# A recommender tower: ten one-hot features instead of eight, one buffer of vectors with placing copies, ids spread two items ahead

## The reference

```python
combined = concatenate([dense[:, None, :], e], axis=1)            # 2048 x 27 x 128
inter = einsum('bnd,bmd->bnm', combined, combined)[:, I, J]       # pairs, 351
h = concatenate([dense, inter, dense], axis=1)                    # 607
h = maximum(h @ W_top1 + b_top1, 0); h = maximum(h @ W_top2 + b_top2, 0); y = h @ W_top3
```

## Time and profile before

| | |
|---|---|
| median of 3 runs | 590.69 us (590.42 to 593.9) |
| the profiled execution | 589.59 us, its span 587.5 us |
| mean granted TensorE clock | 0.916 of full speed |
| busy: PE, DVE, ACT, POOL | 465.1, 317.5, 206.3, 280.9 us |
| DMA, mean | 46 GB/s |

### The profile page before, as it was taken

How to read it: one execution, slowest core, us unless ns; L and a number is a source line. 1 busy time by engine, 2 the same in 40 slices (tenths; PEclk the granted TensorE clock), 3 DMA queues, 4 the chain that set the end, 5 groups by cost and what they waited for, 6 DMA issues and landing times. The chain is left out here.

```text
span 587.5 us, 11290 instructions
## 1 busy us (share of the span) xinstructions
PE 465.1 (79%) x4081; PEld 410.4 (70%) x4081; DVE 317.5 (54%) x733; ACT 206.3 (35%) x708; POOL 280.9 (48%) x298
## 2 busy tenths in 40 slices
PE   1748867898888978797687959879887958886667
PEld 1637756788777977687576858668776857765556
DVE  5445885645566655646465546545665635634140
ACT  2112352333443343335143333423542343334231
POOL 8742345554555545445554555545455545555100
PEclk9999898797899998899799977979899978999689
DMA  8910021111111111111111111111111111111000
GB/s 218 259 39 19 24 73 38 37 42 37 38 37 37 42 42 37 36 40 37 41 37 43 37 32 42 42 43 40 36 38 37 41 37 37 40 38 37 18 1 1
DMA packets 17307, 27.21 MB, mean 46 GB/s; under 512 B 8561, under 2 KB 11121, under 8 KB 17241
## 3 DMA queue, kind: packets, MB, share of 16 engines
q0 software_dynamic: 9216, 18.89, 11.2%
q1 hardware_dynamic: 8034, 7.54, 5.0%
HBM read 26.40 MB, written 0.01 MB: 45 GB/s over the span
## 5 line engine op out<-in xcount | busy, mean ns | idle before, releaser
L271 POOL DMA_INDIRECT rows<-in_tbl,idx x288 | 277.8, 964 | 266.8 <-DMA rows<-in_tbl,idx 161.9
L633 DVE TENSOR_TENSOR onehot<-ids_ps,row_of 125x1024 fp32r<-125x1024 f32 x130 | 153.0, 1218 | 87.9 <-PE ids_ps L341 58.9
L356 PE MATMUL fetch_ps<-onehot,t_hi 125*128 125x256 f32 x512 | 157.1, 331 | 50.9 <-ACT vecs L504 17.4
L356 PEld LDWEIGHTS fetch_ps<-onehot,t_hi 125*128 125x128 f32 x512 | 114.8, 224 | 62.4 <-issue 36.9
L356 PE MATMUL fetch_ps<-onehot,t_lo 125*128 125x256 f32 x512 | 154.0, 326 | 1.3 <-issue 1.3
L691 DVE COPY_PREDICATED inter<-mask,dots_ps 27x64 f32<-27x64 int32 (+2 forms) x512 | 106.0, 207 | 87.1 <-ACT inter L533 72.2
L533 ACT COPY inter<-dots_ps 27x64 f32<-27x64 f32 (+1 forms) x512 | 102.1, 199 | 113.8 <-remote 58.8
L333 PE MATMUL dots_ps<-vecs 128*64 128x54 f32 x2048 | 131.7, 227 | 6.4 <-issue 5.1
L333 PEld LDWEIGHTS dots_ps<-vecs 128*64 128x64 f32 x2048 | 123.8, 141 | 14.2 <-issue 8.1
L356 PEld LDWEIGHTS fetch_ps<-onehot,t_lo 125*128 125x128 f32 x512 | 114.4, 223 | 8.4 <-issue 4.9
L504 ACT COPY vecs<-fetch_ps 128x256 f32<-128x256 f32 x64 | 38.7, 605 | 175.8 <-PE fetch_ps L356 107.7
(11 more groups left out here) (39 smaller groups left out, 162.1 us busy)
## 6 DMA issues: line engine op xcount, KB each, us to landing
rows<-in_tbl,idx POOLq DMA_INDIRECT x288
vecs<-in_tbl SPq DMA_DIRECT2D x8, 448.0 KB
rows<-in_r_dense_features SPq DMA_DIRECT2D x16, 64.0 KB
h_sb<-in_W_top_laid SPq DMA_DIRECT2D x2, 512.0 KB, 3.5
w_sb<-in_W_top SPq DMA_DIRECT2D x1, 512.0 KB
vecs<-in_tbl SPq DMA_DIRECT2D x8, 52.0 KB
idx<-in_ids SPq DMA_DIRECT2D x16, 13.0 KB
h_sb<-in_W_top_laid SPq DMA_DIRECT2D x1, 256.0 KB
```

The costliest lines, as they stand in the source:

```text
L271: nc.gpsimd.indirect_dma_start(out=rows[v % 2][:, s, :], out_offset=None, in_=tables[f - 1][:, :], in_offset=bass.IndirectOffsetOnAxis(ap= ...
L356: last = pe.matmul(fetch_ps, part[0:KP, k, h * KH + t, :], onehot[buf][h][0:KP, t, :], start=(h == 0 and t == 0 and part is t_hi), stop=(h ...
L633: dve.tensor_tensor(onehot[buf][h][0:KP], ids_ps[0:KP].rearrange("p (o r) -> p o r", o=1).to_broadcast([KP, KH, R]), row_of[0:KP, h * KH:( ...
```

## The change

Features 2 and 8, with tables of 1250 rows (10 blocks of 125), are fetched by one-hot too; their items come first and have 20 matmuls. A tile has 16 gathers and 17 transposes left, in groups of 3, 4, 4, 4 and 2 vectors. `vecs` is one buffer for one round; fetched items are copied to a new buffer `found` [128, 10, 256], contiguously, and at the head of the next step ScalarE copies them to `vecs` in two *placing* copies, one per tile (`place`), each after the dots that read that tile's place last and before item 0 is copied to `found`. Groups 0, 2, 4 of a tile are always copied by ScalarE, 1 and 3 by VectorE. The ids of item k + 2 are spread within item k; the first comparison of the next round stands before the last split. Item 3 stands between a tile's transposes 0, 1 and layer 1's last part, items stand around each half of layer 2, and the last two items around layer 3. The second dense weights have their own buffer, so GpSimd no longer waits for their sum; tile 0's groups wait for each other. SP waits for the first two tables' conversion before it loads `W_top1`; the output goes in two DMAs. The diff, its core:

```diff
+SPREAD = (2, 8, 1, 5, 6, 9, 14, 18, 24, 26)
+
+AT_ONCE = 4
 
...
-    groups = [list(range(a, min(a + 4, NR))) for a in range(0, NR, 4)]
+    groups = [list(range(a, b)) for a, b in ((0, 3), (3, 7), (7, 11), (11, 15), (15, 17))]
...
+    KP = 125
+    KT = [tables[f - 1].shape[0] // KP for f in SPREAD]
+    KH = [kt // 2 for kt in KT]
...
-        vecs = [sb(f"vecs{s}", [P, 2, P, NP]) for s in range(2)]
+        vecs = sb("vecs", [P, 2, P, NP])
+
+        found = sb("found", [P, X, R])
...
-        w_dense2 = rows[1][:, NR - 4:NR, :].rearrange("p s d -> p (s d)")
...
+        w_dense2 = sb("w_dense2", [P, H1])
...
+            sp.wait_ge(hi_made, 2)
+            sp.wait_ge(lo_made, 2)
...
+            by_round = out.rearrange("(i r n) o -> o r i n", r=2, n=R)
+            for r in range(2):
+                sp.dma_start(by_round[:, r], y_sb[r * LATE:r * LATE + 1].rearrange("p (i n) -> p i n", n=R)).then_inc(
+                    out_written, 16)
+            sp.wait_ge(out_written, 32)
...
-                    if k == NG - 2 and first and v == 1:
-
-                        pool.wait_ge(dense_w_sum, 1)
...
-                        if not (first and v == 0):
-                            pool.wait_ge(gathered[vv % 2][kk], ii * (32 * n) + (vv // 2 + 1) * 16 * n)
+                        pool.wait_ge(gathered[vv % 2][kk], ii * (32 * n) + (vv // 2 + 1) * 16 * n)
                     pool.sem_inc(groups_begun, 1)
-                    for s in mine:
+                    landed = i * (32 * len(mine)) + v // 2 * (16 * len(mine))
+                    for n, s in enumerate(mine):
                         f = ORDER[s]
+                        if n and n % AT_ONCE == 0:
+
+                            pool.wait_ge(gathered[v % 2][k], landed + 16 * n)
+                            pool.sem_inc(gathers_resumed, 1)
                         nc.gpsimd.indirect_dma_start(
...
-            def fetch_item(i, r, k):
-                spread = {0: 1, 1: 3, 3: 4, 4: 6, 6: 8}
-                fetch(k, *item(i, r, k), spread_of(i, r, spread[k]) if k in spread else None)
+
+            def fetch_items(i, r, *ks):
+                for k in ks:
+                    ahead = {0: 1, X - 1: None}.get(k, k + 2)
+                    fetch(k, *item(i, r, k), spread_of(i, r, ahead) if ahead else None)
...
-                        if k == 4:
+                        if k == X - 4:
                             pe.wait_ge(ident_made, 1)
-                        if k >= 4:
-                            transpose_rows(i, v, (k - 4,))
+                        if k >= X - 4:
+                            transpose_rows(i, v, (k - X + 4,))
                     transpose_rows(i, v, (4,))
-                    fetch_item(i, r, 0)
+                    fetch_items(i, r, 0)
                 dots(i, v, 0, spread_of(i, r, 2))
-                fetch_item(i, r, 1)
-                if prev:
-                    layer1(*prev, 1)
-                    layer1(*prev, 2)
+                fetch_items(i, r, 1)
+                if prev:
+                    layer1(*prev, 1, 2)
                 else:
                     transpose_rows(i, v + 1, (0, 1))
-                fetch_item(i, r, 2)
+                fetch_items(i, r, 2)
                 dots(i, v, 1)
                 if prev:
                     transpose_rows(i, v + 1, (0, 1))
+                fetch_items(i, r, 3)
+                if prev:
                     layer1(*prev, 3)
                 transpose_rows(i, v + 1, (2, 3, 4))
-                fetch_item(i, r, 3)
-                dots(i, v + 1, 0, spread_of(i, r, 5))
-                fetch_item(i, r, 4)
+                fetch_items(i, r, 4)
+                dots(i, v + 1, 0)
+                fetch_items(i, r, 5)
                 if prev:
                     layer2(*prev, 0)
-                fetch_item(i, r, 5)
-                dots(i, v + 1, 1, spread_of(i, r, 7))
-                fetch_item(i, r, 6)
+                fetch_items(i, r, 6)
                 if prev:
                     layer2(*prev, 1)
-                fetch_item(i, r, 7)
+                fetch_items(i, r, 7)
+                dots(i, v + 1, 1)
+                fetch_items(i, r, 8)
                 if prev:
                     layer3(*prev)
+                fetch_items(i, r, 9)
...
-            def copy_fetched(slot, k, m):
+            def copy_fetched(k, m):
                 act.wait_ge(onehot_used, m * 2 + 2)
-                nc.scalar.copy(vecs[slot][:, :, :, NR + k],
-                               fetch_ps.rearrange("p (t b) -> p t b", t=2)).then_inc(fetched, 1)
+                nc.scalar.copy(found[:, k, :], fetch_ps).then_inc(fetched, 1)
 
             def copy_items(i, r, *ks):
                 for k in ks:
-                    copy_fetched((r + 1) % 2, k, item(i, r, k)[0])
+                    if k == 0:
+
+                        act.wait_ge(placed, i * 4 + r * 2 + 2)
+                    copy_fetched(k, item(i, r, k)[0])
+
+            def place(i, r, t):
+                if not (static(i) and i == 0 and r == 0):
+
+                    act.wait_ge(dots_done, i * (8 * UNITS) + r * (4 * UNITS) - (1 - t) * 2 * UNITS)
+                if t == 0:
+                    act.wait_ge(fetched, i * (2 * X) + (r + 1) * X)
+                nc.scalar.copy(vecs[:, t, :, NR:N],
+                               found[:, :, t * P:(t + 1) * P].rearrange("p k b -> p b k")).then_inc(placed, 1)
...
+                    place(i, r, 0)
                     take_vectors(i, v, 0)
+                    place(i, r, 1)
                     copy_items(i, r, 0)
                     take_vectors(i, v, 2, 4)
                     rectify1(*prev, 0)
...
+                    act.wait_ge(lo_made, X)
+                    place(i, r, 0)
+                    place(i, r, 1)
                     take_vectors(i, v, 4)
                     copy_items(i, r, 0)
...
                 if prev:
                     rectify1(*prev, 1, 2)
                 else:
-                    take_vectors(i, v + 1, 1)
+                    take_vectors(i, v + 1, 0)
+                    split(X)
                 copy_items(i, r, 2)
                 take_products(i, v, 1)
                 if prev:
-                    take_vectors(i, v + 1, 1)
+                    take_vectors(i, v + 1, 0)
+                copy_items(i, r, 3)
+                if prev:
                     rectify1(*prev, 3)
                 else:
+                    split(X + 1)
+                split_input(i, v)
+                take_vectors(i, v + 1, 2, 4)
+                copy_items(i, r, 4)
+                take_products(i, v + 1, 0)
+                copy_items(i, r, 5)
+                if prev:
+                    rectify2(*prev, 0)
+                copy_items(i, r, 6)
+                if prev:
+                    rectify2(*prev, 1)
+                else:
                     split(X + 2)
-                split_input(i, v)
-                take_vectors(i, v + 1, 3)
-                copy_items(i, r, 3)
-                take_products(i, v + 1, 0)
-                copy_items(i, r, 4)
-                if prev:
-                    rectify2(*prev, 0)
-                copy_items(i, r, 5)
+                copy_items(i, r, 7)
                 take_products(i, v + 1, 1)
-                copy_items(i, r, 6)
-                if prev:
-                    rectify2(*prev, 1)
+                copy_items(i, r, 8)
                 split_input(i, v + 1)
-                copy_items(i, r, 7)
+                copy_items(i, r, 9)
...
-                    take_vectors(i, v, 1, 3)
-                    compare_items(i, r, 1, 2)
+                    take_vectors(i, v, 1)
+                    compare_items(i, r, 1)
+                    take_vectors(i, v, 3)
+                    compare_items(i, r, 2)
                 else:
-                    compare(0, 0)
+                    compare(0, 0, 0)
                     make_mask()
-                    dve.tensor_copy(ids_t[:, R:B], ids_i[:, R:B]).then_inc(ids_cast, 1)
+                    dve.tensor_copy(ids_t[:, R:B // 2], ids_i[0:X, R:])
+                    dve.tensor_copy(ids_t[:, B // 2:B], ids_i[LATE:LATE + X, :]).then_inc(ids_cast, 1)
                     for k in range(X):
                         split(k)
                         if k + 1 < X:
-                            compare(k + 1, (k + 1) % 2)
-                        if k == 6:
+                            compare(k + 1, k + 1, (k + 1) % 2)
+                        if k == X - 3:
+
+                            dve.wait_ge(lo_made, 6)
                             take_vectors(i, v, 1)
-
                     dve.wait_ge(lo_made, X)
-                    dve.memset(vecs[1][:, :, :, N:], 0.0)
-                    sum_dense_weights()
+                    dve.memset(vecs[:, :, :, N:], 0.0).then_inc(pads_zero, 1)
                     compare_items(i, r, 0)
                     take_vectors(i, v, 3)
                     compare_items(i, r, 1, 2)
+                merge_products(i, v, 0)
+                compare_items(i, r, 3)
```

(77 more changed lines are left out.)

116 lines of the change are left out of this document (59 added, 57 removed).

## The result

The changed kernel takes 609.0 us (median of 4, 605.1 to 611.6), the kernel before, run beside it, 590.6: a ratio of 1.030, 95% interval 1.023 to 1.037. The profiled execution took 607.9 us, its span is 606.4. This holds for the chip of these runs. On another chip the same changed kernel is faster than the kernel before, and that is the main finding.

A forecast was written before the change was run, and what follows sets the result against it. Gathers (67.0 us a step) and TensorE run nearly level before; after, TensorE alone sets the pace at 67.1. Span 587.5 + 18 (start) + 7 (steps) - 5 (end) = 607.5, plus 2.1 around it: 609 us, range 582 to 623.

The forecast's parts named there:

- the start: Two more table conversions before the first tile: tile 0 transposed at 80.4 us instead of 66.3, +14.1 us.
- the first step: Tile 0's to tile 2's transposes: placing copies +1.5, fetching +5.3, less about 3 us of wait; tile 2 18 us later.
- the end: Tile 15's gather waits go, -6 us, and the placing copies give 1 back: -5 us.
- TensorE's work: Per step, eight items of 16 matmuls become eight of 16 and two of 20, less four transposes: +5.3 us.
- Own step before: TensorE's two-tile step in the kernel before, without gather waits and 1.1 us of slow clock: 62.8 us.
- (a): Item 3 between transposes and layer 1's last part covers the wait for vector copies: -1.6 us a step, 0.5 kept.
- (c): Waits for fetched items behind product copies, 2.7 us a step: less cover at the second place, +0.5, up to +0.9.
- (b): Ids two items ahead and next round's comparison moved earlier take the one-hot wait away: -0.8 us a step.
- The placing copy: ScalarE's 128x1280 copy at a step's head takes 1.8 us, between 1.2 and 2.4, adding 0.9 us per step.
- rival (2): Clock: 4.4 us a step of work lost at 1.2 GHz goes with the gather waits; 589 us, chance 0.125.
- Rival (1): Reordering removes 3.6 us a step more of TensorE's waits for other engines; 588 us, chance 0.125.
- (4): Slower still: placing copies at 2.4 us or more and waits at their upper ends; 625 us, chance 0.15.

## Why the prediction was right

The forecast was 609 us and the measured median is 609.0. The mechanism is the one named: the bound passes from the gathers to TensorE, whose step is 67.4 us (forecast 67.1). That it hits to the microsecond is luck. The sum gave a span of 607.5 us and it was 606.4, from terms that were off by more: the start by -6.5 us, the first step by +9.2, the six steps by +1.9 and the end by -5.7.

- *Gathers out of the way*: right. No wait of PE for rows from 140 us on; the last gathers are issued at 543.5, before tile 14 is transposed.
- *TensorE's work, +5.3 us; net of waits +4.3*: near. On the second chip, without stalls and with loosened gathers, the two kernels' steps are 330.3 / 6 = 55.0 and 358.2 / 6 = 59.7 us, a difference of 4.7. TensorE's busy time in six steps on the fourth chip is 302.9 us in the kernel before with loosened gathers, at a granted clock of 1.00, and 335.6 in the changed one, at 0.99: 5.4 a step, for the forecast's 5.3.
- *Own step before, 62.8 us*: not tested where it was read. The 54.2 us of another chip don't refute it, since the changed kernel's step differs by 7.4 between the chips; adding that gives an estimate of 61.6.
- *Waits*: (a) the wait for VectorE's copy went, but group 4's for ScalarE came in both tiles of a step, 20.7 / 6 = 3.4 us where I had 0.9 + 0.5. (c) I kept 3.2 us for fetched items, and 6.9 / 6 = 1.2 was left. (b) 0.6 of the one-hot waits stayed. In sum 5.2 against 4.6 us, besides 2.8 us of short waits put down to "issue".
- *The placing copy*: the upper end, 2.47 us, and not the middle that I took; the row that reads SBUF with a stride (L528) was the one to go by. The Trainium skill's rule (SBUF — State Buffer, The DMA port swizzle), extra cost for every new line of 16 bytes, fits in its direction: 2.47 us for reads 1 KB apart against 1.27 for reads without a gap.
- *The clock*: part of rival (2) did happen. Over the six steps the granted clock is 0.96, before it was 0.92. With +5.3 us of work the busy time grew by only 3.3 a step, so the clock gave back about 2.0 us (an estimate), where I had 1.1. The waits took that back: idle time fell by 1.8 us a step, where I had 2.0 for gathers and 1.0 for the rest. So a step grew by 1.5 us where I had 1.2.
- *The start*: forecast +14.1 for tile 0, measured +7.6. So tile 0 was ready before 75 us, which the prediction had set as a sign of being wrong. The step that failed is that I added two turns to the whole of before's start. That had a stall in it which did not come back:

```profile
32.57 2.35 DVE L633 TENSOR_TENSOR onehot<-ids_ps,row_of 125x1024 fp32r<-125x1024 f32 x2 [7.37 <-remote]
```

  A turn's usual wait there is 2.7 us, so 4.7 us were the stall's. Three of the changed kernel's turns have a shorter wait there, 2.41, 1.65 and 2.11 us, which gives most of the rest. The turns themselves are as worked out: items start at 13.16 and 20.58, 7.4 us for ten blocks (7.5 by my terms).
- *The first step*: +13.1 where I had 18 - 14.1 = 3.9. Two placing copies in series are 4.83 us, and dots start 5.2 us after tile 0's transposes instead of 2.4. TensorE is idle for 2.3 us before them, and they ran mostly at the low level of the clock. In the whole first step its busy time is 58.2 us against 48.8 before, 9.3 more where I had 5.3, at a granted clock of 0.83 against 0.86. The changed kernel's stretch of them, granted clock third from the right, is this, where it was 1.00 before:

```profile
79.00:87.00 8.00, 7.89 (x71) 7.46 (x72) 3.89 (x10) 2.89 (x15) 2.99 (x4) 0.57 0.09 26
```

- *The end*: -10.7 against -5. From tile 14's last transpose to tile 15's it is 19.6 us after, 30.3 before: besides the 6.0 us of gather waits another 5 of short waits in that stretch went.
- *The other signs*: no wait for gathered rows, tiles 67.4 us apart, and VectorE and ScalarE busier came as listed. GpSimd's long idle time before a tile's first gathers came only in part, 3.5 to 4.6 us at the last three tiles against 2.3 before, and the profile puts it down to "issue" and not to transposes.
- *Rival (1)* (the reordering takes the waits away, 588 us) did not come on this chip. Of *(4)* the first condition came, a placing copy of over 2.4 us, but not its 625 us. On the fourth chip a case came for which no rival stood: ScalarE's stalls absent altogether. I read ScalarE's idle time with no engine as cause and took it as the kernel's, though it comes and goes with the chip or the occasion. My prediction holds where the stalls are there as in the trace that it was read from.

## What to carry to other kernels

Where two chains have nearly the same length, a change that trades one for the other can be decided by what the trace can't ascribe to the kernel. Look at idle time with no engine behind it, and ask for a second chip before a variant is believed. The kernel that such a trade starts from may allow a better remedy: on the chips without stalls the gathers needed one more group in flight, not two features fewer. And compare variants side by side only: 562 us for an edit that gives nothing looked like a gain of 47.

## What the runs showed of the hardware that was not expected

- Stalls come and go with the chip or the occasion: on the first and third chip, ScalarE stood idle with the releaser "remote" for 51 to 94 us in each of six traced executions, in pauses of mostly 3 to 4 us, and VectorE for 2 to 32 us more; on the second and fourth, in eight traced kernels, not once. The changed kernel took 601 to 609 us with them and 562 without. The kernel before took 587 to 591 us everywhere, as one would expect if its gathers set its pace. The instruction queue moved the same for the same program on each (0.66 MB in 40 packets for the changed kernel). What the stalls are stays open.
- ScalarE copies runs of four floats from PSUM to SBUF in 586 to 589 ns per 128x512 where the run starts at a multiple of 16 bytes, and in 713 where it starts 12 bytes past one, the only other start tried.
- A copy on ScalarE of 128x1280 whose reads are 1 KB apart takes 2.47 us, and 1.27 where it reads without a gap; single-float writes 40 bytes apart cost 625 ns per 256 against 373.
- With one more group of indirect gathers in flight the 288 gathers of a launch are issued 1.25 us apart, with 5 to 6 us in all of waits for gathers to land, against 162 before.
